# A two-layer transformer block on one core: the next batch's normed rows and the batch's probabilities change places

## The reference, cut to what matters

```python
for i in range(DEPTH):                                   # DEPTH = 4
    x = x + self_attention(layer_norm(x, ln1_g[i], ln1_b[i]), Wq[i], Wk[i], Wv[i], Wo[i], bo[i])
    h = layer_norm(x, ln2_g[i], ln2_b[i])
    x = x + (gelu(h @ W1[i] + b1[i]) @ W2[i] + b2[i])    # 256 -> 1024 -> 256
```

## Time and profile before

| what | us |
|---|---|
| median of 3 runs | 3202.05 (3201.18 to 3202.57) |
| the profiled execution | 3197.5 |
| its span in the profile | 3195.3 |
| PE busy | 2854.1 (89%) |
| DVE busy | 1747.0 (55%) |
| ACT busy | 1419.7 (44%) |
| POOL busy | 824.9 (26%) |

### The profile page before, as it was taken

How to read it: one execution, slowest core, us unless ns; L and a number is a source line. 1 busy time by engine, 2 the same in 40 slices (tenths; PEclk the granted TensorE clock), 3 DMA queues, 4 the chain that set the end, 5 groups by cost and what they waited for, 6 DMA issues and landing times. The chain is left out here.

```text
span 3195.3 us, 51547 instructions
## 1 busy us (share of the span) xinstructions
PE 2854.1 (89%) x19618; PEld 1875.6 (59%) x19618; DVE 1747.0 (55%) x5045; ACT 1419.7 (44%) x3115; POOL 824.9 (26%) x829
## 2 busy tenths in 40 slices
PE   6889999877899898999998999989888788799998
PEld 3566666653555565655555555556555444468887
DVE  4666676756566454545454555546576377741112
ACT  4666666623344354544444444444344123232224
POOL 1001111122223232323232322323243121015551
PEclk8999999998999999999999999999999899899999
DMA  4110011012433435353534344443433100022325
GB/s 137 23 20 18 18 18 21 5 55 76 129 99 97 122 113 162 93 145 93 157 111 145 106 132 117 129 128 93 122 91 106 44 7 14 27 73 80 77 81 186
DMA packets 195301, 277.39 MB, mean 87 GB/s; under 512 B 20515, under 2 KB 136230, under 8 KB 190944
## 3 DMA queue, kind: packets, MB, share of 16 engines
q1 hardware_dynamic: 186224, 253.59, 27.7%
q0 software_dynamic: 7680, 16.32, 2.0%
q10 hardware_dynamic: 1152, 4.19, 0.3%
HBM read 151.06 MB, written 119.11 MB: 85 GB/s over the span
## 5 line engine op out<-in xcount | busy, mean ns | idle before, releaser
L1497 PE MATMUL bank<-h2T,w 128*128 128x512 f32 x1024 | 490.1, 634 | 10.5 <-issue 5.4
L1534 PE MATMUL bank<-w,gT 128*128 128x256 f32 x2048 | 474.2, 385 | 0.9 <-ACT gT L1445 0.9
L1534 PEld LDWEIGHTS bank<-w,gT 128*128 128x128 f32 x2048 | 383.5, 191 | 85.0 <-issue 36.3
L1497 PEld LDWEIGHTS bank<-h2T,w 128*128 128x128 f32 x1024 | 200.1, 201 | 250.8 <-issue 248.7
L1445 ACT ACTIVATE gT<-bank,vec 128x512 f32<-128x512 f32 x256 | 175.9, 687 | 385.3 <-PE bank L1497 385.3
L1248 DVE TENSOR_TENSOR y<-y,bank 128x512 f32<-128x512 f32 x64 | 44.0, 687 | 492.1 <-PE bank L1562 492.1
L609 ACT ACTIVATE y<-y,least 128x128 f32<-128x128 f32 (+3 forms) x512 | 252.0, 554 | 52.1 <-DVE least L479 52.1
L1137 POOL TENSOR_TENSOR prob<-prob,rsum 128x512 f32<-128x512 f32 (+1 forms) x256 | 236.0, 949 | 147.8 <-DVE rsum L1303 147.8
L479 DVE CUSTOM_DVE_ANT_0 y<-bank,mask 128x128 f32<-128x128 f32 (+3 forms) x512 | 223.9, 485 | 70.9 <-PE bank L706 69.5
L1468 PE MATMUL bank<-wtok,hT 128*128 128x512 f32 x512 | 235.4, 614 | 23.6 <-ACT hT L1397 22.4
L1391 ACT ACTIVATE prob<-prob,least 128x256 f32<-128x256 f32 (+1 forms) x512 | 239.3, 470 | 14.0 <-DVE least L1280 14.0
(11 more groups left out here) (325 smaller groups left out, 5032.1 us busy)
## 6 DMA issues: line engine op xcount, KB each, us to landing
turned_probs<-prob_blocks SPq DMA_DIRECT2D x128, 256.0 KB, 5.4
probT<-turned_probs SPq DMA_DIRECT2D x32, 1024.0 KB, 6.1
turned_rows<-score SPq DMA_DIRECT2D x252, 128.0 KB, 2.4
score<-turned_rows SPq DMA_DIRECT2D x63, 512.0 KB, 3.8
turned_probs<-prob_blocks SPq DMA_DIRECT2D x128, 192.0 KB, 3.1
probT<-turned_probs SPq DMA_DIRECT2D x32, 768.0 KB, 4.9
w<-in_W SPq DMA_DIRECT2D x8, 1024.0 KB, 8.2
expert_parts<-zeros SPq DMA_DIRECT2D x32, 256.0 KB, 4.6
```

The source lines that it names most:

```text
L1497: ins = nc.tensor.matmul(M[m % 2][:, :], w1[:, k, m * P:(m + 1) * P], h2T[:, k, :], start=(k == 0), stop=(k == KD - 1))
L1534: ins = nc.tensor.matmul(M[i][:, (t % 2) * D:(t % 2 + 1) * D], gT[:, m, t * P:(t + 1) * P], w2[:, m, :], start=(m == 0), stop=(m == MF - 1))
```

## The change

For the next turn's rows (`hT`), on each engine:

- DVE: the statistics go from behind the turned probabilities to in front of the context sum; norm and turn go behind the context sum, in front of `turn_probs(g, 0)`.
- POOL: `rstd` goes from behind `normalise(g, 3)` to behind `normalise(g, 0)`.
- SP: `move_rows1(g + 1)` goes from behind both `move_probs` to in front of them.
- ACT: the two scalings into `hT` go from behind the last gelu to between gelu 3 and gelu 4 (in turn 0, which has no gelu, they stay).

PE's order is the same. The conditions under which each engine waits are the same; they move with the code.

```diff
@@ SP
+                if g + 1 < TURNS:
+                    move_rows1(g + 1)
                 if g < TURNS:
                     move_probs(g, 0)
                     move_probs(g, 1)
                 if 0 < e < DEPTH and b == 1:
                     sp.wait_ge(s["w2_full"], 2 * B * e)
                     load_w2(e)
-                if g + 1 < TURNS:
-                    move_rows1(g + 1)
@@ POOL
-                    for q in range(4):
-                        normalise(g, q)
+                    normalise(g, 0)
                     if g + 1 < TURNS:
                         rstd("stats1", g + 2, "rstd1")
+                    for q in range(1, 4):
+                        normalise(g, q)
@@ DVE
+                    if g + 1 < TURNS:
+                        nxt = c.y[:, (g + 1) % B]
...
+                        stats(nxt, "stats1")
                     context_sum(g)
+                    if g + 1 < TURNS:
...
+                        norm(nxt, "rstd1", g + 2, "norm1")
+                        if g:
+                            turned2_away.wait(dve, 16 * GROUPS * g)
+                        turn_rows("norm1", g + 2)
                     turn_probs(g, 0)
                     invert(g, 2)
                     turn_probs(g, 1)
@@ ACT
+            def rows_away(g):
+                turned1_in.wait(act, 16 * g)
+                gains_in(g, hT[:, :, 1:1 + T], 0, "h1_gain")
...
+                        if m == MF // 2 and g + 1 < TURNS:
+                            rows_away(g + 1)
                         act.wait_ge(s["hidden_full"], MF * (g - 1) + m + 1)
                         nc.scalar.activation(gT[:, m, :], M[m % 2][:, :], ACT.Gelu,
...
-                if g + 1 < TURNS:
-                    turned1_in.wait(act, 16 * (g + 1))
-                    gains_in(g + 1, hT[:, :, 1:1 + T], 0, "h1_gain")
+                if g == 0:
+                    rows_away(1)
```

More of the change, by code:

```diff
@@ L1339, in _ @@
                         modulate(B + last)
-                    context_sum(g)
+                    if g + 1 < TURNS:
+                        nxt = c.y[:, (g + 1) % B]
+                        if g + 1 < B:
+                            dve.wait_ge(s["modulated"], g + 2)
+                        else:
+                            dve.wait_ge(s["w2_added"], 2 * (g + 2 - B))
+                        stats(nxt, "stats1")
+                    context_sum(g)
+                    if g + 1 < TURNS:
+                        if g:
+                            dve.wait_ge(s["rows_turned"], rows_turned(g, True) - 1)
+                        else:
+                            dve.wait_ge(s["turn1_full"], 2)
+                        norm(nxt, "rstd1", g + 2, "norm1")
+                        if g:
+                            turned2_away.wait(dve, 16 * GROUPS * g)
+                        turn_rows("norm1", g + 2)
                     turn_probs(g, 0)
```

## The result

The changed kernel takes 3408.71 us (median of 4 runs, 3405.28 to 3410.97). The kernel before takes 3201.61 us beside it (4 runs, 3193.99 to 3202.57). The ratio is 1.0651 [1.0633, 1.067]: slower by 207 us. The profiled execution took 3410.97 us, with a span of 3408.8 us. The forecast was 3404 us, in a range from 3340 to 3465.

The account below looks back on a forecast made before the run. PE's wait for part 1 of the turned probabilities was taken to bound the kernel. 194 us later landing plus 38 us slow clock less 30 us won made 202, added to the median 3202.05: 3404 us, range 3340 to 3465.

Parts of the forecast that it names:

- What bounds the kernel: PE in the second layer block: its 116.9 us wait for part 1 of the turned probabilities sets the turn's length.
- DVE in front, d: DVE: the context sum ends later by 0.75 us in a plain turn, 1.04 us in a modulated one.
- Norm and turn, 2.74: DVE: norming and turning the next rows behind the context sum takes 2.74 us before SP can start their scatter.
- rival of the locked norm: DVE beside POOL: the norm waits for POOL's second product, 1.0 us more in each of 31 turns, 3435 us; chance 7%.
- SP's order: SP's queue: the rows' scatter and issuing their gather, 3.70 plus 0.42 us, come before part 0's scatter.
- Transfers beside each other: DMA: part 0's scatter beside the rows' gather takes 1.2 us longer, bounds 0.6 to 1.7.
- What part 1's gather gives back: DMA: part 1's gather gains 1.0 us without the rows' scatter behind it, 0.5 us in turns 8 to 23.
- Part 1 later: Part 1 reaches PE 6.35, 5.85 or 6.3 us later by kind of turn, 194 us over 31 turns.
- Clock and `hT`: PE: slow clock after longer waits costs 38 us; vanished waits for `hT`, 22.4 us, and 7.7 us slow clock give back 30.
- New small waits: PE's up-products wait for a sum on DVE, 0.7 us in plain turns, some 4 in modulated, inside part 1's wait.
- The sum: Whole kernel: 194 + 38 - 30 = 202 us slower, 3404 us.
- transfers that overlap for nothing: DMA rival: no contention on part 0, full 1.0 us back on part 1; +118 us, 3320 us; chance 7%.

Follow-up runs that it names:

- e4: Changed kernel, with POOL waiting until the rows are normed before it normalises quarters 1 to 3; 3365.9 us, ratio 1.0546.
- e2: Changed kernel, with the rows' gather issued behind part 0's scatters, so SP isn't held in front of part 0; 3366.2 us, ratio 1.054.
- e3: Changed kernel, with the clearing transfers of turns 8 to 23 moved behind the next turn's first rows' gather; 3391.79 us, ratio 1.0632.
- e9: Changed kernel plus unread PE products before part 1's values, 8 in plain and 4 in modulated turns, none in turn 0; 3345.22 us, ratio 1.0437.
- e10: Kernel before plus unread PE products before part 1's values, 2 in plain and 5 in modulated turns; 3171.2 us, ratio 0.9887.
- e6: Kernel before, with the modulation moved on DVE from in front of the context sum to behind the four turned quarters; 3138.86 us, ratio 0.9824.

## Why the prediction was right, by its own steps

- **What bounds the kernel:** held. Part 1's landing set the turn before, and does after; everything put in front of it came through to the end: 210 us in its sum beside a difference of 207 by the medians and 213.5 by the profiled executions. Of the 116.9 us that it read as the wait for part 1, 1.8 were one wait for part 0. The 22 waits for part 0 in the changed kernel it didn't name; they lie in front of part 1's landing and add nothing.
- **DVE in front, d:** the sizes held, 0.8 for 0.75 and 1.06 for 1.04, but in the plain turns for the wrong reasons. In `e4`, where POOL is out of the way, the context sum ends at 24.39 us, as before: the statistics cost nothing net. I had 0.55 us for them. The 0.8 us are all the context product beside POOL, for which I took 0.2 out of bounds from 0 to 1.5. The reason that I gave, that one POOL product of 1.02 us covers only the start of a 0.4 us instruction, was false: the instruction took 1.19 us. In the modulated turns both terms held: `e4` ends the context sum at 27.8 us, 0.26 later than before for the 0.24 of statistics less modulation, and the product makes 0.8 more.
- **Norm and turn, 2.74:** mis-sized, 3.40. The rival of the locked norm was true, at 0.7 us a turn and not 1.0. It was put at 7% because the norm's rate was taken to tell that POOL couldn't block it. That was the worst step of the prediction: the earlier trace rows gave a rate and said nothing about an overlap, since before no norm ever ran beside POOL. The same rows showed `kneg`, also a `tensor_scalar`, at up to 2580 ns.
- **SP's order:** held, 4.20 us from the rows' scatter to part 0 in the changed kernel for 4.12 in the sum. What the sum couldn't show, `e2` did: even without the wait in the queue about half of it stays, as transfers beside each other take longer.
- **Transfers beside each other:** 0.9 for 1.2 on part 0's scatter, within its bounds. By the medians part 1's scatter is 0.3 us longer, which I had at nothing; summed over the turns it is 3.9 us, so 0.1 a turn.
- **What part 1's gather gives back:** 1.1 and 1.2 for 1.0 where nothing follows it. In turns 8 to 23 nothing for 0.5: the lower bound was the true one, and `e3` shows that the clearing transfers are the reason.
- **Part 1 later:** 210 for 194. Summed over the 31 turns, and not taken from medians, the terms close. Too small were norm and turn (105.6 us for 84.9), SP's hold (133.8 for 127.7) and part 1's scatter (3.9 for 0); the gather gave back 17.2 us for 23. Too large were part 0's scatter (26.1 for 37.2) and the context sum (18.5 for 26.4). That makes +21, +6, +4, +6, -11 and -8, together 18 for the difference of 16.
- **A term on the wrong side of part 1:** the last of these, -8, isn't DVE's. In turns 10, 14, 18 and 26 of the kernel before the projections ran slow behind the long waits for `hT`, and the context sum ended 1.5 to 2.6 us late, 7.8 us in all. The prediction had them, 7.7 us, but under `hT`. With them the landing is 210 for 186, 24 us too little.
- **Clock and `hT`:** in the tails the two terms were +38 and -22.4, and by `e9` and `e10` they are +41 and -44 to -41. Both mechanisms are right. The clock is well sized, `hT` came to half: its waits in the trace, 22.4 us, were what the slow clock had left of them. The net of the tails is 0 for 16.
- **New small waits:** 1.47 us in a plain turn for 0.7 (the sum on DVE comes 0.7 later with the norm), up to 4.7 in a modulated one for some 4. They lie inside the wait for part 1, as said: `e4` cuts them from 69.8 to 31.8 us, and the kernel gains only what part 1 lands earlier; the wait for part 1 takes up the rest (253.9 us).
- **The sum:** 202 for 207 by the medians and 210 in the turns. It was 24 us too small on the landing and 16 too large on the tails. It was closer than its terms deserve, and that is luck.
- **A rival's price:** for transfers that overlap for nothing the plain turn was started from 5.45 us; by the prediction's own d + 5.0 it is 5.8, which makes 3327 us and not 3320. It changes nothing here.

## What to carry to other kernels

Find the chain whose landing PE waits for, and count as lost every microsecond that is put in front of it on any engine or queue, including the instructions that become longer there because another engine now runs beside them. An instruction's rate says nothing about whether it can be locked out; look for the same operation beside the other engine, and where no row shows the pair, let the bound decide and not the argument. And read the same rule backwards: work that stands in front of the bounding chain without need is the gain, here 58 us for moving the modulation. Add such differences up turn by turn: the medians of the modulated turns in `e6` are 4.9 us apart, which would be 54 us in 11 turns, and their sum is 42.8.

## What the runs showed of the hardware that I had not expected

- By the medians, a gather of 1024 KB takes 4.9 to 5.0 us to PE when nothing is issued behind it, 5.2 when the next transfer comes about 2.4 us later, and 6.1 when 512 KB follow at once, be it in four scatters or in two clearing transfers. In between single turns scatter: with the rows 0.93 us behind it the kernel before has 4.91, 4.97 and 6.30 us (turns 9, 17 and 25).
- DVE's norm of 256 elements, at 407 ns, was held to 1127 ns by a POOL product beside it, and a two-tensor instruction of 224 elements went from 0.39 to 1.19 us. The three norms behind the first kept their 407 ns, but POOL had nothing to do beside them: it was idle for 3.20 us. What a longer run of POOL products would do to them isn't shown.
- After 7.88 us of idling PE ran on the lower clock through values and up-products (1.94 and 3.52 us for 1.08 and 1.98, granted clock 0.50 and 0.53) and was back at full speed in the output projection (3.62 us, as in `e9`, granted clock 1.00). Over 31 turns that made 67 us. Products that nobody reads in the idle time took it back (tails of 197.5 us, where 194.7 would be full clock throughout).
- Waits and slow clock hide each other. In the kernel before, 13 waits for `hT` with 22.4 us became 29 waits with 38.1 us once the clock was kept up.
